# A four-layer kernel on one core: a product moved ahead of an unpacking, and five steps of the FP4 layer at other pieces

## What is computed

```python
def dequant_nvfp4(W_packed, scales, block=32):
    low = W_packed & 15
    high = W_packed >> 4 & 15
    idx = jnp.stack([low, high], axis=-1).reshape(N, -1)
    vals = NVFP4_LUT[idx]
    return (vals.reshape(N, K // block, block) * scales[:, :, None]).reshape(N, K)
...
gate = xt @ dequant(gate).T          # 256 -> 2048
up = xt @ dequant(up).T
inter = gelu_tanh(gate) * up
out = inter @ dequant(down).T        # 2048 -> 256
```

## Time and profile before

| | before |
|---|---|
| median of 3 runs | 579.12 us (578.08 to 579.42) |
| the profiled execution | 578.76 us |
| its span in the trace | 576.9 us |
| TensorE busy | 530.1 us, 92% of the span |
| VectorE busy | 472.3 us, 82% |
| ScalarE busy | 387.4 us, 67% |
| GpSimd busy | 379.6 us, 66% |
| granted TensorE clock, mean | 0.993 of full |

### The profile page before, as it was taken

One profiled execution on the slowest core, in us unless ns is written; L12 is line 12 of the kernel. 1 busy time (PEld: TensorE's weight loads), 2 busy tenths in 40 slices (PEclk: granted clock), 3 DMA queues, 4 the chain that ended last, 5 costly groups with the idle time before them and its releaser, 6 DMA issues.

```text
span 576.9 us, 11386 instructions
## 1 busy us (share of the span) xinstructions
PE 530.1 (92%) x4176; PEld 360.2 (62%) x4176; DVE 472.3 (82%) x881; ACT 387.4 (67%) x854; POOL 379.6 (66%) x337
## 2 busy tenths in 40 slices
PE   5679999999999999999997889899999989999894
PEld 2245676666666677666665545466688778656672
DVE  5999999999999999989897886577636996867656
ACT  3876878789777787677768666666676456557221
POOL 2479998899999899878789378721314453534432
PEclk9999999999999999999999999999999999999998
DMA  7135574645554435845245424122110000000002
GB/s 265 39 86 118 131 178 88 143 81 136 105 117 77 86 68 78 197 88 83 56 83 130 117 75 145 30 58 74 38 38 2 2 1 1 0 1 2 1 2 73
DMA packets 98455, 44.62 MB, mean 77 GB/s; under 512 B 88288, under 2 KB 90720, under 8 KB 98400
## 3 DMA queue, kind: packets, MB, share of 16 engines
q1 hardware_dynamic: 97824, 43.64, 32.5%
q10 hardware_dynamic: 576, 0.26, 0.2%
HBM read 21.86 MB, written 1.05 MB: 40 GB/s over the span
## 4 chain that ended last, share of the span: by engine, by line
PE 52%; DVE 25%; POOL 8%; ACT 7%; issue 6%; DMA 1%; ACTq 0%; POOLq 0%; DVEq 0%
PE bank L1606 46%; DVE turned L1178 5%; PE bank L1779 4%; POOL qkl L614 3%; DVE parts L1201 3%; DVE nmax L1166 2%; DVE ol L1215 1%; ACT bank L788 1%; DVE w_all_l L1117 1%; DVE vl L1209 1%; DVE stage L1418 1%; DMA ln_b<-in_bT 1%; DVE turned L1377 1%; POOL rstd L635 1%; DVE nrm L1064 1%
## 5 line engine op out<-in xcount | busy, mean ns | idle before, releaser
L1606 PE MATMUL bank<-xTh,w_all_h 128*128 128x512 f16 (+2 forms) x392 | 130.6, 333 | 11.1 <-DVE w_all_l L1117 4.8
L1606 PE MATMUL bank<-xTh,w_all_l 128*128 128x512 f16 (+2 forms) x392 | 130.3, 332 | 0.0
L1606 PE MATMUL bank<-xTl,w_all_h 128*128 128x512 f16 (+2 forms) x392 | 130.3, 332 | 0.0
L614 POOL TENSOR_TENSOR qkl<-turned,qkh 128x512 f16<-128x512 f32 (+1 forms) x44 | 55.1, 1253 | 98.9 <-ACT qkh L918 98.6
L562 POOL TENSOR_TENSOR rr<-turned 64x512 f32<-64x512 f32 x62 | 88.5, 1428 | 16.5 <-DVE turned L1178 12.6
L788 ACT ACTIVATE bank<-bank,nmax 128x128 f32<-128x128 f32 (+3 forms) x128 | 64.1, 501 | 33.3 <-DVE nmax L1166 32.4
L563 POOL TENSOR_TENSOR rr<-turned 64x512 f32<-64x512 f32 x62 | 80.9, 1305 | 3.6
L570 POOL TENSOR_TENSOR qkl<-rr,qkh 128x512 f16<-128x512 f32 x62 | 71.6, 1162 | 16.8 <-ACT qkh L810 14.3
L918 ACT ACTIVATE qkh<-turned 128x512 f16<-128x512 f32 (+1 forms) x44 | 27.7, 629 | 59.6 <-DVE turned L1377 59.6
L1201 DVE SCALAR_TENSOR_TENSOR parts<-bank,rscaled,parts 128x128 f16<-128x128 f32 (+3 forms) x128 | 64.1, 540 | 2.1 <-ACT parts L799 2.1
L1606 PEld LDWEIGHTS bank<-xTh,w_all_h 128*128 128x128 f16 (+1 forms) x392 | 38.4, 98 | 39.3 <-issue 9.5
(11 more groups left out here) (228 smaller groups left out, 1468.6 us busy)
## 6 DMA issues: line engine op xcount, KB each, us to landing
stage<-in_per_head SPq DMA_DIRECT2D x16, 512.0 KB, 4.3
xa<-in_codes SPq DMA_DIRECT2D x32, 128.0 KB, 2.8
stage<-in_packed SPq DMA_DIRECT2D x12, 256.0 KB, 2.9
stage<-in_scales SPq DMA_DIRECT2D x12, 256.0 KB, 3.5
pT<-parts SPq DMA_TRANSPOSE x128, 2.8
stage<-in_w1T SPq DMA_DIRECT2D x2, 512.0 KB, 3.9
rope<-in_ropes SPq DMA_DIRECT2D x1, 512.0 KB, 7.1
x<-in_x SPq DMA_DIRECT2D x1, 512.0 KB, 6.9
```

The source lines that it names most:

```text
L614: pool.tensor_tensor(il[n % 2][0:rows, :], inter[0:rows, n % 2, :], ih[n % 2][0:rows, :], ALU.subtract).then_inc(g_il, 1)
L1606: last = pe.matmul(dst, l, r, start=start and i == 0, stop=stop and i == 2, skip_group_check=skip)
```

## The change

It does five things, all in the run. No instruction is added or taken away.

1. `product_of(1)` stands on VectorE ahead of the unpacking of pair 2, and behind the sums of the attention. Before, the unpacking and the statistics of the other sequence came first.
2. GpSimd scales block 4 behind `il(1)` and no longer behind `il(0)`, so that blocks 4 and 5 follow each other. Block 8 is scaled behind `il(6)` (before, `il(5)`), and block 9 behind `il(7)` (before, `il(6)`).
3. ScalarE makes the high part of block 8 behind `ih(7)` (before, `ih(6)`) and that of block 9 behind `ih(8)` (before, `ih(7)`). The low parts on VectorE follow them, a piece later each.
4. The table entries of the fourth layer stand behind pieces 3, 8, 10 and 12 (before, 4, 6, 8 and 11), two entries, four instructions, each time.
5. The statistics of x of the other sequence are taken on VectorE behind product 6 (before, behind product 7).

```diff
--- before.py
+++ after.py
@@ -54,9 +54,9 @@
 Q_COLS = 512
 Q_PIECES = 3 * MLP // Q_COLS
 UNPACK_AT = {2: 3, 4: 4, 7: 5}
-SCALED_AT = {0: 4, 1: 5, 3: 6, 4: 7, 5: 8, 6: 9, 8: 10, 9: 11}
-HIGH_AT = {0: 3, 1: 4, 2: 5, 4: 6, 5: 7, 6: 8, 7: 9, 9: 10, 10: 11}
-ENTRIES_AT = {4: 0, 6: 2, 8: 4, 11: 6}
+SCALED_AT = {1: (4, 5), 3: (6,), 4: (7,), 6: (8,), 7: (9,), 8: (10,), 9: (11,)}
+HIGH_AT = {0: 3, 1: 4, 2: 5, 4: 6, 5: 7, 7: 8, 8: 9, 9: 10, 10: 11}
+ENTRIES_AT = {3: 0, 8: 2, 10: 4, 12: 6}
 FP4_AS_FP8 = 64.0
 DW = 1024
 FT = D // P
@@ -654,8 +654,8 @@
                     rstd_of(0, 1, "y")
                 if m == 7:
                     rstd_of(0, 1, "x")
-                if m in SCALED_AT:
-                    scaled(SCALED_AT[m])
+                for j in SCALED_AT.get(m, ()):
+                    scaled(j)
             for m in range(M_TILES):
                 low_inter(RUN2 + m)
                 if m == 0:
@@ -1440,6 +1440,7 @@
                     low_fp4(2)
             product_of(0)
             attention_sums(1)
+            product_of(1)
             dve.wait_ge(t_pv, UNITS - 1)
             unpacked(2)
             signed(2)
@@ -1451,7 +1452,7 @@
                         entries_hit(HIT_AT[n], part)
 
             for m in range(M_TILES):
-                if m:
+                if m > 1:
                     product_of(m)
                 if m == 1:
                     lut_halves()
@@ -1459,7 +1460,7 @@
                     shifted(0, 1, "y")
                 if m == 5:
                     added(0, 1)
-                if m == 7:
+                if m == 6:
                     spread_of_x(0, 1)
                 if m == 10:
                     shifted(0, 1, "x")
```

## The result

| | before | changed |
|---|---|---|
| median | 579.12 us (5 runs, 578.08 to 579.63) | 581.64 us (5 runs, 580.98 to 582.71) |
| the profiled execution | 578.76 us | 580.98 us |
| its span | 576.9 us | 578.8 us |
| granted TensorE clock, mean | 0.993 | 0.990 |

A forecast was written before the change was run, and what follows sets the result against it. TensorE, busy 92% of the span, was taken as the bound, with 6.5 us of waits to win. Wins of 4.8 us against losses of 5.4 to 5.5 gave +0.6, a median of 579.7 us, range 577.6 to 581.6.

The forecast's parts named there:

- Step 1: Before `down(1)`: product 1 starts at 329.93 instead of 331.93, so TensorE's wait of 1.82 us is gone.
- Step 2: Before `down(2)`: unpacking 1.74 us later delays block 4, `high(4)` and gelu(2); TensorE waits 3.1 us, `down(2)` at 340.7.
- Step 3: Before `down(4)`: entries behind piece 3 take 0.96 us in front of gelu(4); `down(4)` at 349.6, +2.0.
- Step 4: Before `down(5)`: block 7's halves, the addition, `low(6)` and `il(5)` queue, 5 x 1.07 us; `down(5)` at 354.9, +2.9.
- Step 5: Block 8 behind `il(6)`: the 2.44 us of waits before `down(6)` and `down(7)` vanish; `down(7)` at 362.7, +0.5.
- The statistics of x at no cost: At piece 6 the statistics of x are covered and cost nothing; without this cover they would cost 1.8 us.
- Step 6: Block 9 behind `il(7)`: GpSimd's queue ends with `il(8)` at 367.3; `down(8)` at 367.4 after a 0.8 us wait, -0.1.
- Step 7: Behind block 9: waits of 0.4 us each before `down(9)` and `down(10)`, which stands at 376.0.
- A: VectorE and GpSimd meetings along the run do not come: -3.7 us, 576.0; chance of over 1.16 us faster 0.16.
- B: Block 11's late loads hold gelu(7), then product 7 and `il(7)`: +3 us, 582.4; chance 0.05.
- C: One more VectorE and GpSimd meeting of 1.07 us, at steps 4, 6 or 7: +1.7 us, 581.4; chance 0.17.
- D: Late unpacking and earlier product 1 cancel to within tenths: 579.1 us; counted within the forecast's chance of 0.62.

The follow-up runs named there:

- the front half: Only product 1 ahead of the unpacking and block 4 behind `il(1)`, rest as before, against the kernel before: 582.24 against 579.49 us, ratio 1.0053.
- product 1 alone: Kernel before with only product 1 moved ahead of the unpacking of pair 2, block 4 left behind `il(0)`: 581.67 against 578.97 us, ratio 1.0046.
- the second group: The changed kernel run once more, unaltered, against the kernel before: 581.49 against 579.12 us, ratio 1.0038.
- the filling matmuls: Changed kernel plus eight matmuls on zeros between up(3) and `down(2)`, against the kernel before: 580.30 against 579.49 us, ratio 1.0029.

## Why the prediction was wrong, by its steps

The forecast was 579.7 us, 577.6 to 581.6, with 0.22 for slower. The median of 581.64 lies just above the range. The forecast's own positions give 376.0 - 375.3 = +0.7 at `down(10)`, its sum of waits +0.6; the difference is rounding. Times below are measured ones less the 0.30 us.

**Step 1, product 1 first: right.** The product began at 330.02 (forecast 329.93), the wait of 1.82 is gone, `down(1)` at 333.62.

**Step 2, the unpacking waits: right up to gelu(2), and then the step that failed.** Block 4 began at 333.15 (333.1), `high(4)` at 335.34 (335.3), gelu(2) at 337.35 (337.25). But the prediction sent product 2 on behind gelu at once. It had put down no meeting for the small instructions of lines 1351 to 1356, which stood in front of `low(3)` and product 2 and had taken half a microsecond in before. Since block 5 now followed block 4 directly, they met three halves of GpSimd's pairs in a row, and product 2 came at 338.71 instead of about 337.85. **The term "waits 3.1 before `down(2)`" was 4.0.** With the small instructions gone it was 3.10, as the experiment shows. The page "SBUF — State Buffer" of the Trainium skill, section "Who interferes with whom", counts the cast and the tensor_scalar among the instructions that can, under conditions, take the shared pair. The rows agree: the cast's 0.17 became 1.02. The prediction's own reading of the rule, "instructions with two operands in SBUF", left them out, though it had listed the integer instruction of 336.56 (1.19 instead of 0.28), which has one operand in SBUF, as held.

**The half clock: not foreseen at all,** neither as a term nor as a rival, though a wait of over 3 us was forecast. `down(3)` was at 347.00 instead of 345.0 and `down(4)` at 350.89 instead of 349.6. Of the 2.0 at `down(3)`, 0.83 was there at `down(2)` already; the half clock added the rest, 1.56 us over the free pace where a wait of 0.4 was forecast.

**Step 3, the entries behind piece 3:** their 0.96 us were right (344.36 to 345.31 on ScalarE, in the trace's own times). TensorE was later than they were, so they held nobody.

**Step 4, five holds in a row: the right number for another reason.** `down(5)` was forecast at 354.9 and stood at 354.91. But block 7 began at 350.59, 1.0 us late, and met nothing: its pair took 2.16, which the prediction had named as a sign against it. The addition then waited for its end, `il(5)` for the addition, and `low(6)` for `il(5)`: 350.59 + 4 x 1.07 = 354.87. A delay of 1.0 and a hold fewer cancelled for TensorE. They did not for VectorE: `low(6)` came last instead of fourth, and product 6 was at 355.85 instead of 354.3.

**Step 5, block 8 behind `il(6)`: right for TensorE,** `down(6)` and `down(7)` without a wait, at 358.82 and 362.80 (358.8 and 362.7). But the slack that it counted on behind `il(6)` was used up: `il(6)` ended at about 358.4 instead of 356.9. "The statistics of x at no cost" was neither shown nor refuted.

**Step 6, block 9 behind `il(7)`: right in its length, wrong in its start.** GpSimd has hardly a gap from 357.57 to `il(8)`'s end at 368.85, in the trace's own times. What came in 1.5 late at `il(6)` went out 1.2 late at `il(8)`: the wait before `down(8)` was 1.89 in starts where 0.8 was forecast.

**Step 7, waits of 0.4 and 0.4: right,** 0.37 and 0.38.

So the mechanism, a queue between VectorE and GpSimd, was the right one, and the term mis-sized was the wait before `down(2)`. Of the 1.2 us between the forecast +0.6 and the trace's +1.83, taking out the small instructions gives back 0.76 and leaves the end at +1.07. The other 0.5 stays with the half clock still there. Whether it is the half clock's is not shown: with the clock full and the small instructions in, the end is at +1.75, and no run has both the clock full and the small instructions out.

**The medians lie higher than the traces:** +2.5 and +2.4 against +1.8. About half of the gap lies outside the span. In every execution on record of before, of the front half and of product 1 alone, the time is 1.80 to 1.94 us longer than the span; in every execution of the change, and of all other versions, it is 2.18 to 2.30 us longer. These others are the ones in which the table entries and the high parts of blocks 8 and 9 stand elsewhere. The forecast added nothing for this 0.35 us, and no run shows where it comes from. Between the spans themselves the medians differ by 1.95 us in the second group (579.25 against 577.3), close to the trace. What is left scatters with the clock: in 56 executions of before, the 12 with a mean clock of 0.990 to 0.992 took 580.0 us on average, the 16 with 0.995 or 0.996 took 578.5. That goes together; what causes what was not tested.

**The rivals.** A (no meetings, -3.7) fell: every pair above shows them. B (late loads hold gelu(7)) didn't come: ScalarE went from to_bytes (357.40, own times) to gelu(7) (358.44) with no idle time. (With the small instructions behind product 2 it did wait 0.70 us for scales there, with the filling matmuls 0.55, but gelu(7) then waited for TensorE, so that the loads held nothing.) C had nearly the right end, +1.7, but put its extra meeting at steps 4, 6 or 7; it was at step 2, and of small instructions that no rival named. D (nothing moves) fell: the late unpacking and the early product don't cancel, the one led to a wait of 4.0 and the other won 1.8.

## What to carry to other kernels

When an order is moved, list every instruction between the moved one and the next consumer, the tiny ones too, and charge each up to a full hold of the other engine where the two now overlap: here three instructions on 8 columns were held for 2.2 us together. Where a change puts two short waits of TensorE together into one long wait, look at what the clock does behind it, and count that as a case of its own. When medians and traces disagree, look first at what lies outside the span. And taking a wait away in front by delaying a step that feeds three engines can cost more than the wait. The version that gained 2.9 us left the product and the unpacking where they were and moved steps around them.

## What the runs showed of the hardware

- **A small instruction waits out the other engine's hold.** A cast of 128x8 took 0.17 us in before and 1.02 beside GpSimd's scaling, two tensor_scalars of 64x8 0.34 and 1.68. Both ended just behind an end of GpSimd's 1.07 us halves.
- **The clock of TensorE fell after idle times of 2.68, 2.91, 3.10 and 3.84 us,** after dense matmuls, and did not after 1.56, 1.88 and 2.11 us (the last behind filling matmuls). There is no sharp line: behind one and the same idle time of 2.64 us, at 26 us, it fell in nine traces and not in three. In four of the seven traces with a fall in the run it fell while TensorE still stood, in three only after `down(2)` had begun, by up to 0.7 us. It came back by itself under dense work. The half clock covered 2.7 to 3.4 us of matmuls in six traces, and 6.0 in one.
- **Half a clock need not cost half the time.** With 3.3 us of it TensorE lost 0.83 us at the next `down` against the trace with the clock full, and 0.08 us at the end, since the waits behind it took up the rest. This is one trace against one.
